# Another order in memory for the two tensors that the second convolution of an attention block reads

## What is computed

```
x = x + dwconv3x3(x)                                   # "pos", first convolution
n = layernorm(x);  q, k, v = n@q_w, (n@k_w)*scale, n@v_w   # 8 heads of 8 channels
a_w = softmax(q.k over the 56 columns of a row + mask_w);   r = a_w @ v
a_h = softmax(q.k over the 56 rows of a column + mask_h);   o = a_h @ r
o = o + dwconv5x5(v)                                   # "lepe", second convolution
x = x + o @ out_w;  x = x + gelu(layernorm(x) @ fc1_w) @ fc2_w
```

## Time and profile before

| | us |
|---|---|
| median of 3 runs | 2260.62 (2260.05 to 2273.13) |
| profiled execution, its own time | 2255.95 |
| span from first to last instruction in it | 2254.1 |
| busy in the span: PE, PEld | 1902.4, 1490.7 |
| busy in the span: DVE, ACT, POOL | 1446.1, 1217.8, 1203.9 |
| DMA queue that SP feeds: packets, MB, share of the 16 engines | 683580, 311.51, 63.3% |

### The profile page before, as it was taken

How to read it: one execution, slowest core, us unless ns; L and a number is a source line. 1 busy time by engine, 2 the same in 40 slices (tenths; PEclk the granted TensorE clock), 3 DMA queues, 4 the chain that set the end, 5 groups by cost and what they waited for, 6 DMA issues and landing times. The chain is left out here.

```text
span 2254.1 us, 89480 instructions
## 1 busy us (share of the span) xinstructions
PE 1902.4 (84%) x34766; PEld 1490.7 (66%) x34766; DVE 1446.1 (64%) x2251; ACT 1217.8 (54%) x2081; POOL 1203.9 (53%) x1820
## 2 busy tenths in 40 slices
PE   4865722899999999998999999999959858499998
PEld 4855721577777777766767676677639757377776
DVE  4566874677767777765666666666654424588785
ACT  3554644455545555554555555555525448488887
POOL 6576964555555545543555455454544425366664
PEclk8877855899999999999999999999979968699999
DMA  9667464678777777777777777777748868455553
GB/s 131 106 137 175 138 198 135 152 165 173 174 163 169 168 169 169 168 170 162 168 174 173 172 173 163 169 167 163 166 81 139 159 135 196 119 135 134 131 133 83
DMA packets 713879, 346.81 MB, mean 154 GB/s; under 512 B 613396, under 2 KB 672532, under 8 KB 713604
## 3 DMA queue, kind: packets, MB, share of 16 engines
q1 hardware_dynamic: 683580, 311.51, 63.3%
q0 software_dynamic: 28864, 30.98, 5.1%
q10 hardware_dynamic: 1160, 0.13, 0.0%
HBM read 105.39 MB, written 102.76 MB: 92 GB/s over the span
## 5 line engine op out<-in xcount | busy, mean ns | idle before, releaser
L856 DVE TENSOR_REDUCE att_mm<-att_s_ps 128x8 f32<-128x448 f32 x896 | 558.3, 624 | 383.3 <-PE att_s_ps L661 382.5
L779 ACT ACTIVATE att_prob<-att_st_ps 128x448 f32<-128x448 f32 x896 | 486.2, 543 | 454.6 <-PE att_st_ps L691 452.7
L704 PEld LDWEIGHTS att_pv_ps<-att_vx,att_prob 128*56 128x56 f32 x14336 | 519.7, 132 | 126.1 <-ACT att_prob L779 3.8
L704 PE MATMUL att_pv_ps<-att_vx,att_prob 128*56 128x18 f32 x14336 | 492.0, 201 | 3.0 <-ACT att_prob L779 2.4
L661 PE MATMUL att_s_ps<-att_kx,att_q_unit 120*56 120x448 bf16 x1792 | 328.4, 363 | 30.5 <-DMA att_q_unit<-att_qk_hi 23.7
L686 PE MATMUL att_st_ps<-att_mvt,set_both 122*56 122x448 bf16 x1792 | 323.9, 357 | 22.2 <-DMA att_mvt<-att_mneg 21.2
L541 POOL COPY att_vx<-att_vf 56x224 f32<-56x224 f32 x512 | 182.3, 386 | 274.7 <-PE att_pv_ps L704 262.5
L691 PE MATMUL att_st_ps<-att_qx,att_k_hi 128*56 128x448 bf16 x1792 | 322.5, 355 | 0.0
L691 PE MATMUL att_st_ps<-att_qx,att_k_lo 128*56 128x448 bf16 x1792 | 320.4, 353 | 0.0
L556 POOL DMA_DIRECT2D att_mvt<-att_mneg x256 | 137.5, 541 | 308.7 <-ACT att_mneg L772 293.1
L547 POOL DMA_DIRECT2D att_qx<-att_q_hilo x512 | 244.9, 486 | 17.5 <-issue 5.6
(11 more groups left out here) (208 smaller groups left out, 3304.5 us busy)
## 6 DMA issues: line engine op xcount, KB each, us to landing
att_xt<-xn_chunks SPq DMA_DIRECT2D x128, 196.0 KB, 3.7
att_k_hi<-att_qk_hi SPq DMA_DIRECT2D x128, 196.0 KB, 3.7
att_k_lo<-att_qk_lo SPq DMA_DIRECT2D x128, 196.0 KB, 4.4
att_qx<-att_q_hilo POOLq DMA_DIRECT2D x512, 49.0 KB, 3.4
pos_x<-in_x_dram SPq DMA_DIRECT2D x128, 105.0 KB
lepe_x<-v_scratch SPq DMA_DIRECT2D x128, 105.0 KB
x_scratch<-pos_x SPq DMA_DIRECT2D x128, 98.0 KB
xn_chunks<-pos_xrt SPq DMA_DIRECT2D x16, 784.0 KB, 5.2
```

The costliest lines, as they stand in the source:

```text
L704: ins = pe.matmul(pv_ps[v % 2][64 * h:64 * h + L, at:at + 18], prob[t % 4][:, 4 * h + a, :], vx[v][:, VW * j + 36 * a + 18 * h:VW * j + 36 ...
L779: act.activation(prob[t % 4][:, :, :], st_ps[t % 2][:, 0:S8].rearrange("p (s q) -> p s q", q=L), ACT.Exp).then_inc(exp_done, 1)
L856: dve.tensor_reduce(mm[v % 2][:, NH * j:NH * j + NH], s_ps[j % 2][:, 0:S8].rearrange("p (s k) -> p s k", k=L), AX.X, ALU.max).then_inc(max ...
```

## The change

v (`v_scratch`) and the attention (`attention`) are kept as image, column, row modulo 4, block of four rows, channel. For one column and one r, 14 x 64 floats are now contiguous, 3584 bytes, and this is what a partition of the second convolution reads. The row attention's result stays as it was. What follows from it:

- `load` and `load_add` of the second convolution read whole pieces.
- In the row attention a pair is made of the neighbouring lines 2j and 2j + 1, so that one half of the partitions has rows 0 and 2 of four and the other rows 1 and 3. `store_v` is four DMAs instead of two, by row modulo 4.
- `normalise` in the row attention is two instructions, one for each line of a pair.
- In the column attention ACT's exponential reads the 56 queries of its input in the order "modulo four, block" (a step of four elements in PSUM) and writes them contiguously, so that a partition of the result is a row in the new order and `store_o` needs as many DMAs as before.
- Storing and loading of v have a semaphore each (`v_st`, `v_io`).

```diff
-        o_sb = [sb(f"o_sb{u}", [128, 2, PAIRS, 32], F32) for u in range(2)]
+        o_sb = [sb(f"o_sb{u}", [128, LINES, 32], F32) for u in range(2)]
+        v_st = [sem(f"v_st{u}") for u in range(2)]
...
             def load_v(i, v):
-                wait(sp, v_io[u], dma_count(i, v, 32) - 32)
+                if i.known and i.at == 0 and v < 2:
+                    sp.wait_ge(v_st[u], 64 * NCH // 2)
+                wait(sp, v_io[u], dma_count(Image(i.at, True), v, 32) - 32)
...
             def store_v(i, v):
                 u = v % 2
                 wait(sp, v_sb, cnt(i, v, 1, 1))
-                dst = chunk_tokens(v_d, i, v, True)
                 for r in range(2):
-                    sp.dma_start(dst[:, PAIRS * r:PAIRS * r + PAIRS, :],
-                                 vf[u][64 * r:64 * r + L, :].rearrange("p (j c) -> p j c", c=C)).then_inc(v_io[u], 16)
+                    src = vf[u][64 * r:64 * r + L, :].rearrange("p (j c) -> p j c", c=C)
+                    for e in range(2):
+                        j0 = (PAIRS * v + e) % 2
+                        at, n = (PAIRS * v + j0) // 2, (PAIRS - j0 + 1) // 2
+                        sp.dma_start(v_d[i.at, :, 2 * e + r, at:at + n, :], src[:, j0::2, :]).then_inc(v_st[u], 16)
 
             def store_o(i, v):
-                dst = chunk_tokens(row_d if i.rows else att_d, i, v, i.rows)
+                if i.rows:
+                    dst = chunk_tokens(row_d, i, v, True)
+                else:
+                    dst = att_d[i.at, LINES * v:LINES * v + LINES].rearrange("l r j c -> (r j) l c")
                 for h in range(2):
-                    sp.dma_start(dst[:, :, 32 * h:32 * h + 32],
-                                 o_sb[u][64 * h:64 * h + L].rearrange("p r j c -> p (r j) c")).then_inc(o_out[u], 16)
+                    sp.dma_start(dst[:, :, 32 * h:32 * h + 32], o_sb[u][64 * h:64 * h + L]).then_inc(o_out[u], 16)
...
-                            ins = pe.matmul(pj[0][64 * r:64 * r + L, C * j:C * j + C], x[:, PAIRS * r + j, :],
+                            ins = pe.matmul(pj[0][64 * r:64 * r + L, C * j:C * j + C], x[:, 2 * j + r, :],
...
-            def line_of(v, r, j):
-                return LINES * (v % 2) + PAIRS * r + j
+            def line_of(i, v, r, j):
+                return LINES * (v % 2) + (2 * j + r if i.rows else PAIRS * r + j)
...
-                act.activation(prob[t % 4][:, :, :],
-                               st_ps[t % 2][:, 0:S8].rearrange("p (s q) -> p s q", q=L),
-                               ACT.Exp).then_inc(exp_done, 1)
+                out, src = prob[t % 4][:, :, :], st_ps[t % 2][:, 0:S8].rearrange("p (s q) -> p s q", q=L)
+                if not i.rows:
+                    out = out.rearrange("p s (r j) -> p s r j", r=RB)
+                    src = src.rearrange("p s (j r) -> p s r j", r=RB)
+                act.activation(out, src, ACT.Exp).then_inc(exp_done, 1)
...
             def values(i, v):
-                wait(dve, v_io[u], dma_count(i, v, 32) - 32)
+                wait(dve, v_st[u], dma_count(i, v, 64) - 64)
...
             def normalise(i, v):
-                dve.tensor_tensor(o_sb[u][0:120].rearrange("p r j (a d) -> p (j a) r d", a=4), got[:, :, :, 0:8],
-                                  sums.unsqueeze(3).to_broadcast([120, 4 * PAIRS, 2, 8]), ALU.mult).then_inc(norm_done, 1)
+                if i.rows:
+                    at = o_sb[u][0:120].rearrange("p (j r) (a d) -> p j a r d", r=2, a=4)
+                    for r in range(2):
+                        ins = dve.tensor_tensor(at[:, :, :, r, :], got[:, :, r, 0:8].rearrange("p (j a) d -> p j a d", a=4),
+                                                sums[:, :, r].rearrange("p (j a) -> p j a", a=4).unsqueeze(3).to_broadcast(
+                                                    [120, PAIRS, 4, 8]), ALU.mult)
+                    ins.then_inc(norm_done, 1)
+                else:
+                    dve.tensor_tensor(o_sb[u][0:120].rearrange("p (r j) (a d) -> p (j a) r d", r=2, a=4),
+                                      got[:, :, :, 0:8],
+                                      sums.unsqueeze(3).to_broadcast([120, 4 * PAIRS, 2, 8]), ALU.mult).then_inc(norm_done, 1)
...
         def out_rows(dram, b, r, s):
-            return dram[b].rearrange("(j r) (s w) c -> r s w j c", r=RB, s=2)[r, s]
+            if pos:
+                return dram[b].rearrange("(j r) (s w) c -> r s w j c", r=RB, s=2)[r, s]
+            return dram[b, WH * s:WH * s + WH, r]
 
         def in_rows(dram, b, r, s):
-            return dram[b].rearrange("(j r) w c -> r w j c", r=RB)[(r + 2) % RB, 26 * s:26 * s + 30]
+            if pos:
+                return dram[b].rearrange("(j r) w c -> r w j c", r=RB)[(r + 2) % RB, 26 * s:26 * s + 30]
+            return dram[b, 26 * s:26 * s + 30, (r + 2) % RB]
...
-    v_d = scratch("v_scratch", [B, H, W, C], F32)
+    v_d = scratch("v_scratch", [B, W, RB, JB, C], F32)
-    att_d = scratch("attention", [B, H, W, C], F32)
+    att_d = scratch("attention", [B, W, RB, JB, C], F32)
```

More of the change, by code:

```diff
@@ L523, in _ @@
                 sp.wait_ge(o_out[u], 32 * NCH)
-                sp.wait_ge(v_io[u], 32 * NCH)
+                sp.wait_ge(v_io[u], 32 * NCH // 2)
         @block.gpsimd
@@ L533, in build_vx @@
                 else:
-                    wait(pool, v_io[u], dma_count(i, v, 32))
+                    wait(pool, v_io[u], dma_count(Image(i.at, True), v, 32))
                 wait(pool, pv_done, cnt(i, v, 7, -21))
@@ L659, in scores @@
                 for r in range(2):
-                    ln = line_of(v, r, j)
+                    ln = line_of(i, v, r, j)
                     ins = pe.matmul(s_ps[j % 2][64 * r:64 * r + L, 0:S8].rearrange("p (s k) -> p s k", k=L),
```

## The result

| kernel | median, us | ratio to before, 95% interval |
|---|---|---|
| before | 2260.34 (2254.7 to 2273.13) | |
| changed | 2306.33 (2301.9 to 2310.23) | 1.0189 (1.0147 to 1.0231) |

The change makes the kernel 46 us, 1.9%, slower. The forecast was 2261 in a range of 2239 to 2285: it was wrong, and the rival "SP takes over the row attention" (2297) is what happened. The span of the profiled execution is 2300.1 us, 46.0 more than before.

The account below looks back on a forecast made before the run. The prediction took a ring of engines to bound the second convolution, and PE, with SP close behind, the row attention. Loads -11, SP's issues +11 and normalise +1 made +1 on the median: 2261 us, range 2239 to 2285.

Parts of the forecast that it names:

- SP takes over the row attention: Row attention: rival that the added issues cost up to 1.5 us a period, 36 us more, 2297; chance 0.12.
- I let half of the 2.2 come back: Row attention: shrinking stretches return half of SP's added 2.2 us a period, leaving 0.36 a period, 11 us more.
- if nothing comes back, 21.0, or 1.5 times 31 = 46 more: Row attention: upper bound of SP's cost, with no stretch shrinking; a period of 21.0 us, 46 us more.
- what SP and the DMAs need: Attention: a period of about 19.4 us, with the rows 0.1 to 0.2 us above it.
- The second convolution, -11 forecast: Second convolution: longer pieces in the loads of v save 11 us (4 to 19).
- First stall: Second convolution: quicker issue and landing of the fourth image's loads save 3 us (1 to 5).
- Three turns: Second convolution, ring of engines: a store landing in about 4.0 us saves 2.2 a turn, 6.6 in all (3 to 12).
- Last load: Second convolution: from the last load to the relay, 6.4 us becomes 5.7 (0 to 1.5 less).
- Normalise: Row attention, DVE: the second instruction costs 0.16 us 64 times, nearly all hidden; 1 us more (0 to 10).
- The exponential: Column attention, ACT: stepping through PSUM by 4 elements costs 0 us; 13 if the cover were gone.
- The packets and the semaphores: Whole kernel: 617367 packets if the stores of v keep 256 bytes; the semaphores cost nothing.
- The rule on issues: Row attention, SP: by the skill's rule the four issues cost nothing, 2251; the rival with that time had chance 0.25.

Follow-up runs that it names:

- before_v4: Kernel before with v stored in four DMAs a chunk instead of two, to the old places in 256-byte pieces; 2302.05 us, ratio 1.0207.
- before_tiny: Kernel before with two more DMAs a chunk of the row attention on SP, each of one 256-byte piece; 2288.7 us, ratio 1.0126.
- before_v4_big: before_v4 with v's four stores going to 768 or 1024 bytes in a row of memory instead of 256; 2301.84 us, ratio 1.0196.
- v4_o_long: before_v4 with the row attention's result stored in pieces of 1792 bytes instead of 128, as many DMAs; 2281.73 us, ratio 1.0106.
- after_v_act: Changed kernel with v's four stores issued by ACT, one behind each of four exponentials, instead of SP; 2260.64 us, ratio 1.0013.
- after_v2: Changed kernel with v stored in two DMAs a chunk instead of four, to places of the old pattern; 2260.55 us, ratio 1.0011.

## Why the prediction was wrong

**What failed is one term: "I let half of the 2.2 come back."** The 2.2 us a period for four more issues was right (2.3 by the sums above): less the 0.7 us that SP stood idle it is 1.5, and the period grew by 1.54. Nothing came back. This can be read directly: take SP's DMA instructions of a period, less what they would take at the shortest time seen for each. That stretch is 4.4 us before, 4.6 in the changed kernel, 4.7 in before_v4, 4.5 in before_tiny and 4.8 in before_v4_big. I had read SP's stretched issues (1.47 us for a pair that can take 0.91) as the DMA engines being behind, and had taken it that they catch up when SP slows down. In the changed kernel the DMA share did fall, from 0.76 to 0.71, and the groups of v are still stretched. before_v4_big takes away five sevenths of the pieces of v and nothing shrinks; v4_o_long removes most of those of the row result and about 1 us of a period shrinks, while the longest stretch stays in its place. The bound that I kept for this case, "if nothing comes back, 21.0, or 1.5 times 31 = 46 more", is the measured 21.11 and 48. It had a chance of 0.12 because I argued the recovery from one resource, without a row that showed stretches shrinking.

**The period of SP.** I put "what SP and the DMAs need" at 19.4 and the rows just above it. after_v_act shows the two bounds apart: with v's stores elsewhere SP has 4.7 us of idle time, and the period is still 19.68, 19.3 of it PE's work. Before the change both engines stood within 0.7 us of each other, so an addition of 2.2 on one of them was bound to show. The columns' 19.4, with two loads of v a chunk in the place of the two stores, had already said that SP has next to no room.

**The second convolution, -11 forecast, -4.8 measured in this pair of traces, -3.4 by the means.** By its parts:

- First stall: 3 forecast. DVE starts on what is loaded there 110.3 us into the stage before (1780.31 - 1670.0) and 107.3 after (1827.94 - 1720.6): 3.0, right. In the other traces it is 109.8 to 112.2 with the old layout and 107.6 and 108.9 with the new, so this gain is clear of the scatter.
- Three turns: 6.6 forecast, 3.0 measured (59.3 to 56.3). The store's landing came down to 4.4 to 4.55 us, not to 4.0. And I had taken its present length from 5.1 and 6.4; in the three turns it was 5.2, 5.0 and 6.4, on average 5.5. So each turn gains 1.05 in this pair of traces, which is within the scatter of the three turns (53.3 to 59.3 us with the old layout, 54.9 to 56.3 with the new). How much of the 6.6 is real, and why most of it is not, stays open.
- Last load: 0.7 forecast, 6.4 to 5.8 measured.
- After it 1.9 us are given back, in the part where PE is fed. I have no experiment on that.

The rate behind it was off as well: I took 376 GB/s from the stores in pieces of 1568 bytes, and the loads in 3584 reach 214. Eight loads are 0.86 MB (not 0.84), and SP took 3.45 us for them at its quickest, so it could not have fed more than 249 GB/s. But 214 is below that, and the DMA share in the same window is 0.97, so the trace does not tell whether SP or the DMA engines set the 214.

**Normalise, +1 forecast, about +4 measured:** the instruction cost 147 ns more as estimated (160), but somewhat less of it seems to have been hidden; inside the bound of 10.

**The exponential, 0 forecast.** It is

```profile
L790 ACT ACTIVATE att_prob<-att_st_ps 128x448 f32<-128x448 f32 x896 | 485.5, 542 | 461.1 <-PE att_st_ps L698 459.3
```

against 543 ns. Half of these are in the rows, where nothing steps; the 376 in 1120 to 1640 us, columns alone, also have a mean of 542, against 543 before. So this step of four elements in PSUM costs ACT nothing. The Trainium skill's rule on lines of 8 bytes in PSUM ("SBUF — State Buffer", "Door 1: The DMA port swizzle") names matmuls as what such patterns slow down. The prediction carried it over to an ACT read, where it would have made the exponential longer; for that read this trace does not agree.

**The packets and the semaphores** came as forecast, and `store_o` and the line order cost nothing that can be told from noise: after_v2 contains them and stands at 2260.6.

**The rule on issues.** In before_tiny four issues a period with next to nothing to move cost 30 us, in before_v4 44 us. The Trainium skill's sentence that the sequencer's time is usually small relative to the DMA ("DMA: Bandwidth & Descriptors", "Issuing engines are not separate DMA queues") may hold for one DMA; it would have given 2251 here. The trace does not agree for a queue that issues nearly without pause: what counts there is the sum of issues in a period, not their ratio to the transfers.

## What to carry to other kernels

Count the issue slots of a DMA queue like the instructions of an engine: add up a period of the issuing queue from its timeline, subtract its idle time, and price every added DMA at its full issue time with its register instructions, here 0.45 us for one piece and just under 0.6 for the stores of v. Don't let stretches "come back" unless a row shows them shrinking. Before a gain from better pieces is counted, look at what is queued ahead of what on the same queue: moving one issue ahead of eight gave 13.5 us in the second convolution (29 with what it gave in the first), the better pieces 3 to 5 with that queue as it was and 13 without.

## What the runs showed that I had not expected

- By the medians a DMA of one piece occupies SP three quarters as long as one of 168 or 224: the tiny one of before_tiny has a median of 237 ns, the store of v in before_v4 320.
- A pair of stores takes 2.6 us in the period shown behind four copies of k and 0.9 in the other chunk, with 784 pieces each or with 56.
- Pieces 14 times as long (3584 against 256 bytes) raised a load's rate by 15% only, from 186 to 214 GB/s. SP issued the 64 loads in 30.47 us, 0.48 us for each 105 KB.
